# A two-pass graph layer on one core: another order of its opening, on four queues

## The reference, cut to what matters

```python
h = jnp.maximum(_layernorm(x), 0.0)                  # 5120 x 64
u = par_u[0] * par_u[1] * (diag_u[:, None] * h[:nu] @ W_u) + h[:nu]
i = par_i[0] * par_i[1] * (diag_i[:, None] * h[nu:] @ W_i) + h[nu:]
e = jnp.concatenate([u, i], axis=0)
t = adj.T @ e                                        # first pass over adj
g = adj @ t                                          # second pass over adj
mu, var = g.mean(-1), g.var(-1)
out = x + (g - mu) * rsqrt(var + 1e-5) * ln_gamma + ln_beta + h
```

## Time and profile before

| | us |
|---|---|
| median of 3 runs | 379.37 |
| lowest, highest | 378.68, 379.71 |
| profiled execution, its own time | 380.46 |
| its span, first to last instruction | 378.5 |
| PE busy | 367.7 (97%) |
| DVE busy | 252.6 (67%) |
| ACT busy | 73.9 (20%) |
| POOL busy | 23.1 (6%) |

### The profile page before, as it was taken

The page is one execution under the profiler, slowest core; times in us unless marked ns, Lnnn a source line. Parts: engine busy times, 40 slices in busy tenths (PEclk is TensorE's granted clock), DMA queues, the critical chain, the costliest instruction groups (busy, mean ns, idle before and its releaser), DMA issues.

```text
span 378.5 us, 9719 instructions
## 1 busy us (share of the span) xinstructions
PE 367.7 (97%) x4328; PEld 193.7 (51%) x4328; DVE 252.6 (67%) x242; ACT 73.9 (20%) x212; POOL 23.1 (6%) x29
## 2 busy tenths in 40 slices
PE   6988999999999999999999999999999999999994
PEld 4656364544644564365446445643654464456332
DVE  5996997939826942993398269529933982632376
ACT  5763022020230022002201300220022013002321
POOL 2029100000000000000000000000000000000035
PEclk9899999999999999999999999999999999999999
DMA  8999999999999899699959996996999599939003
GB/s 303 425 416 420 377 425 422 419 421 419 421 419 421 313 426 426 249 383 422 425 194 417 424 395 211 422 425 272 360 426 425 203 401 427 416 136 410 14 10 130
DMA packets 19602, 133.13 MB, mean 352 GB/s; under 512 B 2176, under 2 KB 2560, under 8 KB 3712
## 3 DMA queue, kind: packets, MB, share of 16 engines
q1 hardware_dynamic: 19296, 132.48, 85.7%
q10 hardware_dynamic: 288, 0.39, 0.3%
HBM read 131.55 MB, written 1.31 MB: 351 GB/s over the span
## 4 chain that ended last, share of the span: by engine, by line
PE 86%; DMA 6%; DVE 4%; issue 2%; SPq 2%; ACT 0%; DVEq 0%
PE t_acc L636 42%; PE h_acc L665 35%; PE h_acc L649 8%; DMA natural<-adj_rows 6%; SPq L205 1%; PE t_acc L702 1%; DVE var L417 1%; DVE strips L454 1%; DVE scaled L578 1%; SPq L202 0%; DVE natural L562 0%; PE h_acc L716 0%; DVE scaled L571 0%; DVE centred L467 0%; DVE xs L593 0%
## 5 line engine op out<-in xcount | busy, mean ns | idle before, releaser
L454 DVE STREAM_TRANSPOSE strips<-natural 128x2048 f32<-128x2048 f32 x76 | 168.2, 2274 | 47.6 <-PE h_acc L665 47.6
L636 PE MATMUL t_acc<-natural,e 128*64 128x256 f32 x1600 | 176.3, 380 | 1.9 <-DMA natural<-adj_rows 1.9
L636 PEld LDWEIGHTS t_acc<-natural,e 128*64 128x64 f32 x1600 | 115.2, 137 | 64.2 <-issue 9.5
L665 PE MATMUL h_acc<-strips,centred 32*64 32x512 f32 x2432 | 133.3, 589 | 0.2 <-DVE strips L454 0.2
L665 PEld LDWEIGHTS h_acc<-strips,centred 32*64 32x64 f32 x2432 | 53.0, 132 | 79.4 <-issue 78.3
L334 ACT COPY t_high<-t_acc 64x256 f32<-64x256 f32 x20 | 7.4, 368 | 210.3 <-PE t_acc L636 210.3
L462 DVE TENSOR_TENSOR t_sum<-t_acc,t_high 64x256 f32<-64x256 f32 x20 | 8.2, 412 | 60.1 <-ACT t_high L334 59.8
L649 PE MATMUL h_acc<-cols,centred 128*64 128x512 f32 x160 | 38.3, 599 | 0.8 <-ACT centred L342 0.8
L341 ACT COPY centred<-centred 32x384 f32<-32x384 f32 (+2 forms) x60 | 24.2, 403 | 71.4 <-DVE centred L475 70.9
L342 ACT COPY centred<-centred 32x128 f32<-32x128 f32 (+2 forms) x60 | 23.9, 398 | 0.0
L289 POOL TENSOR_TENSOR scaled<-scaled,smalls 128x512 f32<-128x512 f32 x2 | 2.5, 1274 | 327.4 <-DVE scaled L578 327.4
(11 more groups left out here) (53 smaller groups left out, 76.2 us busy)
## 6 DMA issues: line engine op xcount, KB each, us to landing
natural<-adj_rows SPq DMA_DIRECT2D x100, 1024.0 KB, 11.3
cols<-adj_cols SPq DMA_DIRECT2D x20, 1024.0 KB, 13.0
natural<-adj_last SPq DMA_DIRECT2D x4, 1024.0 KB, 7.2
out<-xs SPq DMA_DIRECT2D x5, 256.0 KB, 2.0
xs<-x SPq DMA_DIRECT2D x3, 256.0 KB, 9.4
xs<-x ACTq DMA_DIRECT2D x1, 256.0 KB, 3.9
smalls<-small SPq DMA_DIRECT2D x1, 214.5 KB, 3.6
xs<-x ACTq DMA_DIRECT2D x1, 128.0 KB, 2.9
```

The source lines that it names most:

```text
L454: nc.vector.transpose(strips[:, a, :, m].rearrange("p c t i -> p t c i"), natural[:, a, m].rearrange("p t (c j) -> p t c j", j=Q)).then_in ...
L636: last = nc.tensor.matmul(t_acc[D * s:D * (s + 1), a, 0:WIDE], e[:, GT * m + 2 * k + s, :], natural[:, a, m, HALF * s + k], start=(m == 0 ...
L665: last = nc.tensor.matmul(h_acc[D * s:D * (s + 1), q], t[part, a, b, u, :], rows, start=(isinstance(g, int) and g == 0 and b == 0 and u == 0),
```

## The change

Four lists get another order, and no instruction is added or left out.

- SP: the load of unit 4 goes ahead of `natural(1, 0)`. Groups 2, 3 and 4 of panel 0 are loaded in one run, then those of panel 1 (before: group 2 of both panels, then 3 and 4 of panel 0, then of panel 1).
- ACT and DVE: the steps of the six units are interleaved in another way. DVE turns `natural(0, 2)` ahead of `keep_t(0, 0)` instead of behind it.
- PE: units 0, 1 and 2 are turned first, then all three multiplied by W. The first products of group 1 are done for panel 1 ahead of panel 0, as are the second halves of group 0. `second_strips` of panel 0 goes ahead of its `second_loaded`.
- `firsts_0` follows PE's new order.

```diff
--- before.py
+++ after.py
@@ -152,8 +152,8 @@
         def firsts_0(g, m):
 
             if g == 0:
-                return (1, 3, 5, 6, 7)[m]
-            return (2, 4, 8, 9, 10)[m]
+                return (2, 4, 5, 6, 7)[m]
+            return (1, 3, 8, 9, 10)[m]
 
         def part_bank(m):
 
@@ -213,14 +213,13 @@
             sp.dma_start(smalls[:], small).then_inc(s_small, 16)
             load_natural(0, 0)
             load_x(3)
+            load_x(4)
             load_natural(1, 0)
-            load_x(4)
             load_x(5)
-            for m in (1, 2):
-                for g in range(2):
-                    load_natural(g, m)
             for g in range(2):
-                for m in (3, 4):
+                load_natural(g, 1)
+            for g in range(2):
+                for m in (2, 3, 4):
                     load_natural(g, m)
             load_cols(0)
             for g in range(2, PANELS):
@@ -352,25 +351,25 @@
 
             square(0)
             positive(0)
+            square(1)
             std(0, 4)
-            square(1)
+            positive(1)
+            square(2)
+            std(1, 4)
+            positive(2)
             layer_input(0)
-            positive(1)
-            std(1, 4)
-            square(2)
-            positive(2)
+            std(2)
             layer_input(1)
+            positive(3)
             square(3)
-            std(2)
+            square(4)
             std(3)
-            positive(3)
-            square(4)
+            positive(4)
             layer_input(2)
-            positive(4)
+            square(5)
             std(4)
+            positive(5)
             layer_input(3)
-            square(5)
-            positive(5)
             std(5)
             layer_input(4)
             layer_input(5)
@@ -495,47 +494,47 @@
             row_sums(1)
             sum_squares(0, 4)
             centre_rows(1)
+            row_sums(2)
+            centre_rows(2)
             deviation(0)
-            row_sums(2)
             sum_squares(1, 4)
             scale_by_diag(0)
-            centre_rows(2)
-            embed_part(0)
-            deviation(1)
-            embed(0)
+            sum_squares(2)
             row_sums(3)
             centre_rows(3)
-            scale_by_diag(1)
-            sum_squares(2)
-            sum_squares(3)
-            embed_part(1)
-            embed(1)
+            deviation(1)
+            embed_part(0)
+            embed(0)
             row_sums(4)
             centre_rows(4)
+            row_sums(5)
+            sum_squares(3)
+            scale_by_diag(1)
+            embed_part(1)
             deviation(2)
+            embed(1)
             scale_by_diag(2)
-            deviation(3)
+            centre_rows(5)
             embed_part(2)
-            row_sums(5)
             sum_squares(4)
             embed(2)
+            deviation(3)
+            sum_squares(5)
             scale_by_diag(3)
-            centre_rows(5)
             deviation(4)
+            turn_strips(0, 0, 0, 0)
+            scale_by_diag(4)
             embed_part(3)
-            scale_by_diag(4)
+            deviation(5)
             embed(3)
-            sum_squares(5)
-            turn_strips(0, 0, 0, 0)
-            deviation(5)
             embed_part(4)
+            embed(4)
             scale_by_diag(5)
-            embed(4)
             embed_part(5)
             embed(5)
             turn_strips(0, 0, 0, 1)
+            turn_strips(0, 0, 0, 2)
             keep_t(0, 0)
-            turn_strips(0, 0, 0, 2)
             turn_strips(0, 0, 0, 3)
             for m in range(TURNED):
                 turn_strips(1, 1, 0, m)
@@ -728,34 +727,32 @@
 
             pe.wait_ge(s_idle, 1)
             warm(WARM)
-            turn_unit(0)
-            turn_unit(1)
-            weights(0)
-            turn_unit(2)
-            weights(1)
-            weights(2)
+            for u in range(3):
+                turn_unit(u)
+            for u in range(3):
+                weights(u)
+            turn_unit(3)
             pe.wait_ge(s_e, 1)
             first(0, 0, 0, 0, range(2))
-            turn_unit(3)
+            turn_unit(4)
             first(1, 1, 0, 0, range(2))
-            turn_unit(4)
             weights(3)
+            weights(4)
             pe.wait_ge(s_e, 2)
+            first(1, 1, 0, 0, range(2, HALF))
+            turn_unit(5)
             first(0, 0, 0, 0, range(2, HALF))
-            first(1, 1, 0, 0, range(2, HALF))
             pe.wait_ge(s_e, 3)
+            first(1, 1, 0, 1)
             first(0, 0, 0, 1)
-            turn_unit(5)
-            first(1, 1, 0, 1)
-            weights(4)
             weights(5)
             for m in (2, 3, 4):
                 pe.wait_ge(s_e, m + 2)
                 first(0, 0, 0, m)
             for m in (2, 3, 4):
                 first(1, 1, 0, m)
+            second_strips(0, 0).then_inc(s_strips_done, 1)
             second_loaded(0, 0, 0)
-            second_strips(0, 0).then_inc(s_strips_done, 1)
             for g in range(2, PAIRED):
                 step(g, g % 2, g // 2)
             second_strips(PAIRED - 1, 1).then_inc(s_strips_done, 1)
```

## The result

| | before | changed |
|---|---|---|
| median | 379.01 us (20 runs) | 377.82 us (20 runs) |
| lowest, highest | 378.68, 379.71 | 377.42, 379.13 |
| ratio, 95% interval | | 0.9972 (0.9964 to 0.9980) |
| profiled execution, its own time | 380.46 | 378.12 |
| its span | 378.5 | 376.2 |

The forecast was 377.8 us for the median and 0.41% less than before. The median is 377.82, but the gain by the ratio is 0.28% (0.20 to 0.36), 1.06 us; the two medians are 1.19 us apart. The kernel before has itself a median of 379.01 over 20 runs, against the 379.37 of three that the forecast started from. A second comparison gave 0.9966 (0.9953 to 0.9978), 1.3 us. Whether the gain is over 0.3% hangs on which of the two is taken.

A forecast was written before the change was run, and what follows sets the result against it. Bound: PE's own work from 39.65 us; before it, a chain through the load of `natural(0, 4)`. F(2,0) at 36.33 + 7.06 + 1.77 = 45.16, 1.55 earlier: 380.46 - 1.55 = 378.9 profiled, 377.8 median; range 377.2 to 379.8.

The forecast's parts named there:

- Loads: Opening loads of adj: `natural(0, 4)` lands at 27.0 instead of 29.49 us, the last tile `natural(1, 4)` still at 34.4.
- F(1,4): PE's first product of panel 1, group 4: starts at 34.6 us after its load, issued out by 36.33.
- The cover is thin: each tenth beyond 0.65 goes on the path: DVE's and ACT's results for panel 0 are ready 0.6 to 0.7 us ahead of PE at 36.33.
- first rival: DVE takes the load's place: `keep_t` and the last transpose end over 0.65 us late; 379.0 us, chance 0.14.
- F(2,0): PE's first product of panel 2, group 0: starts at 45.16 us against 46.71, 1.55 earlier.
- `e` in time: DVE's opening list: `e` of unit 3 at 22.9 us, 3.0 ahead of its limit; second transpose still at 25.85.
- The swap of S and L: Panel 0 on PE: `second_strips` starts at 36.33 us and takes 7.06, `second_loaded` behind it takes 1.77.
- What the swap delays: `load_cols(2)` and panel 3's five loads on SP issue later: cost 0, slacks of 2.0 and 2.1 us left.
- fourth rival: Later first products wait for saturated loads, so the gain is given back: 379.4 us, chance 0.06.
- The clock: PE in the opening: half clock expected until about 15 us rather than 11.8, then 1.00.
- nothing after F(0,2) moves, because DVE's list is the slower one until then: Half clock until about 15 us costs nothing behind PE's first product of panel 0, group 2, since DVE is slower.
- The second and third rivals: Clock falls while PE follows loads, 378.7 us, chance 0.04; clock stays low in the opening, 379.9 to 381.0, chance 0.10.

The follow-up runs named there:

- second comparison: The changed kernel, nothing edited, timed again beside the kernel before: 0.9966 (0.9953 to 0.9978).
- first changed trace: Profiled execution of the changed kernel in the main result, against the kernel before; own time 378.12 us.
- second trace: Another profiled execution of the changed kernel, nothing edited; own time 379.02 us.
- POOL held: The changed kernel plus one wait, so that POOL's second additions start behind `keep_t` of panel 0: 0.9960 of the kernel before, 377.65 us.

## Why the prediction was right, and where it was not

- *The number.* 377.8 forecast, 377.82 measured. That the two agree so closely is luck: the gain was 1.06 us by the ratio and 1.19 by the medians, not 1.55, and the base was 0.36 us lower than the three runs had shown, which made up for it. "Faster by over 0.3%" had 0.58; the first comparison is just inside 0.3%, the second just outside.
- *Loads.* Right in kind. In the trace of after `natural(0, 4)` lands two and a half us ahead relative to the last tile of all, and F(0,4) no longer bounds anything. The absolute times came from one execution whose stream began a us later than that of the first changed trace and then, like that one, had one gap of about 4.0 us in it: 34.6 for F(1,4), against 33.1 and 33.56 in the two traces of the changed kernel. This is the step that was mis-sized. Shifting it by 1.0 to 1.5 leaves DVE's times, and so turns the next step round.
- *"The cover is thin: each tenth beyond 0.65 goes on the path."* This is what failed as a statement of which engine is late. DVE's tiles were ready at 35.5 (forecast 35.6), but PE was free already at 35.05, and waited 0.55 us, in the second trace 1.13. The first rival's place was right; its mechanism too, in part: one of the five instructions of `keep_t` got longer, from 1.10 to 1.70, not all five. Its price was 0.55 to 1.1 us against a start that had itself moved ahead. The slow products with W, which no rival had put on DVE's list at this size, were the other source of the first trace's wait. With POOL held and no slow products S had no wait, and F(2,0) came 0.67 us earlier than in the first trace.
- *`e` in time.* Right in its place: the second transpose was forecast for 25.8 and started at 25.12 with x early, 26.17 with x late. The load of x had been taken as fixed; it is not: unit 3 landed at 8.18 and 9.81.
- *The swap of S and L.* S to F(2,0) was reckoned at 7.06 + 1.77 = 8.83 and is 44.43 - 35.60 = 8.83. Its price by itself was not asked for in the prediction: 3.3 us lost on the old opening, because it puts the later of two waits first and PE's clock then falls.
- *What the swap delays.* Right, nothing: PE never waits for a load behind 44 us, and the constant 333.6 us behind F(2,0) excludes the fourth rival.
- *The clock.* The forecast that it would be at half until 15 was wrong: in the first trace W's 16 products took 3.35 us from 7.89 on, against 2.05 from 14.21 (rows after, above), and from 11.07 PE has its full pace. So there was a slow stretch, but it ended before 11.1, no later than the 11.8 of before. It is read from the pace alone: the profile's granted clock for 7.89 to 11.30 says 1.00. The second trace has none (eight products in 1.06 us from 7.49 on). What failed here is "nothing after F(0,2) moves, because DVE's list is the slower one until then": the slow products held that very list up by 0.5 us, and F(0,2) started at 23.35 against 22.84 in the trace without them. The second and third rivals did not happen. Behind 15 us, a clock brought down by PE's waiting, at a price, was seen only with the swap alone.

Shares, from the ratios: loads 0.13%; the turn nothing on top of them; the opening 0.12% on top of both (the intervals overlap), nothing by itself; the swap 0.14% on top of these (not told apart from zero), 0.20% with POOL held (the intervals touch). Only the loads' share and the whole are clear of zero. The parts don't add up singly; by the traces each takes away the wait that hides behind the one before, but the runs are too close to one another to show this part by part.

## What to carry to other kernels

An execution's first loads may be late by over a microsecond, so a sum that sets one engine's path against a load's landing to a tenth needs several traces of the kernel before; or it must say which of the two is late in each case. When several reorderings meet at one wait, price each alone as well: here one that helps in company costs 3.3 us by itself. Look at what a third engine does beside a short critical instruction: on the old kernel, one wait on POOL gave about half as much as the whole change (0.15% against 0.28).

## What was not expected of the hardware

- The first tile of 1 MB, issued at 1.6 us, landed between 7.4 and 9.5 us in the twelve traces in which it was issued third; the last one of the opening, in all fourteen, between 33.0 and 34.5.
- A DVE instruction with two inputs in SBUF (32 x 512) took 0.68 us alone and 0.94 to 1.71 beside POOL's additions of 128 x 512, while DVE's transposes kept their 2.2 us pace beside them. The Trainium skill's "GPSIMD Engine Reference", Specifications, names this case of two SBUF inputs; the runs agree, and put 0.3 to 1.0 us on it.
- In the first changed trace matmuls with W started 0.21 us apart up to 10.5 us and 0.11 apart behind it, which cost 0.5 us on DVE's list; the profile's granted clock says 1.00 for all of it.
- After 2.79 us of waiting on PE, at 38 us, 3.4 us at a granted clock of 0.50, with 1.7 us lost. None after waits of 1.32 at 27 us, or of 1.09, 1.13 and 1.27 at 36 to 38 us in other traces. In the opening it also fell with shorter waits: to 0.50 at 8.4 us in the kernel before, where 1.34 was the longest.
